# Another operation order and another PSUM bank table for a fused tokenizer, attention and feed-forward kernel

## The reference

```python
h = tok(x)                                   # 16x16 patches: layernorm(768), @ W (768x256) + b, layernorm(256) -> (64, 196, 256)
h = concatenate([h, txt], axis=1)            # (64, 273, 256)
h = h + attn(_layernorm(h), Wq, bq, Wk, bk, Wv, bv, Wo, bo)   # 16 heads of 16, over the 273 tokens reshaped by the projection
h = h + ffn(_layernorm(h), W_r, W_k, W_v, mu_r, mu_k)         # sigmoid(xr @ Wr.T) * (relu(xk @ Wk.T)**2 @ Wv.T), xr/xk mix each token with the one before
```

## Time and profile before

| | |
|---|---|
| median of 3 executions | 1610.56 us (1608.76 to 1613.27) |
| the profiled execution's own time | 1609.15 us |
| span in its trace | 1607.4 us, mean granted PE clock 0.968 |
| busy share | PE 90%, PEld 86%, DVE 79%, ACT 69%, POOL 59% |
| DMA | 227.67 MB moved, mean 142 GB/s |
| chain that ended last | PE 65%, SP queue 8%, issue 6%, DMA 5%, DVE 3% |

### The profile page before, as it was taken

One profiled execution on the slowest core, in us unless ns is written; L12 is line 12 of the kernel. 1 busy time (PEld: TensorE's weight loads), 2 busy tenths in 40 slices (PEclk: granted clock), 3 DMA queues, 4 the chain that ended last, 5 costly groups with the idle time before them and its releaser, 6 DMA issues.

```text
span 1607.4 us, 53715 instructions
## 1 busy us (share of the span) xinstructions
PE 1450.4 (90%) x18762; PEld 1378.2 (86%) x18762; DVE 1264.3 (79%) x3171; ACT 1113.4 (69%) x2230; POOL 947.0 (59%) x1428
## 2 busy tenths in 40 slices
PE   4687899999989999998999899999999999897866
PEld 4676899899989999898989899998988999897755
DVE  5566798888888888887988688888888788886753
ACT  4554687777777787776777678777777777765643
POOL 3342376566667666565667566666766566664546
PEclk8788899999999999999999999999999999999998
DMA  5267987997878887987888798798888689868760
GB/s 140 63 125 126 139 154 147 150 159 158 151 144 162 157 156 154 149 152 145 155 147 157 140 151 154 162 150 147 155 158 156 137 152 148 160 123 127 123 100 29
DMA packets 702660, 227.67 MB, mean 142 GB/s; under 512 B 617470, under 2 KB 673854, under 8 KB 702394
## 3 DMA queue, kind: packets, MB, share of 16 engines
q1 hardware_dynamic: 702394, 224.23, 77.3%
HBM read 121.64 MB, written 89.64 MB: 131 GB/s over the span
## 4 chain that ended last, share of the span: by engine, by line
PE 65%; SPq 8%; issue 6%; DMA 5%; DVE 3%; POOL 1%; ACT 1%; DVEq 0%; POOLq 0%; ACTq 0%
PE bank L1066 33%; PE bank L1146 13%; PE bank L1103 4%; PE bank L1124 4%; SPq L547 4%; DMA qk<-qkv_dram 3%; PE bank L1134 3%; SPq L519 2%; PE bank L1111 2%; PE bank L1180 2%; PE bank L1162 1%; PE bank L1194 1%; DMA on<-o_dram 1%; SPq L556 1%; PE bank L1153 1%
## 5 line engine op out<-in xcount | busy, mean ns | idle before, releaser
L1066 PE MATMUL bank<-wqkv,xnT 128*126 128x384 f32 (+1 forms) x1728 | 357.8, 347 | 6.9 <-issue 6.8
L1146 PE MATMUL bank<-wtok,xT 128*98 128x258 f32 x2304 | 315.7, 293 | 13.3 <-DVE xT L789 9.3
L1146 PEld LDWEIGHTS bank<-wtok,xT 128*98 128x98 f32 x2304 | 294.8, 172 | 18.9 <-DVE xT L789 11.3
L1066 PEld LDWEIGHTS bank<-wqkv,xnT 128*126 128x126 f32 (+1 forms) x1728 | 293.6, 186 | 10.6 <-issue 8.0
L689 POOL TENSOR_TENSOR mixp<-mixf,mixp 128x364 fp32r<-128x364 f32 x192 | 185.5, 977 | 166.0 <-ACT mixp L1040 158.7
L866 DVE TENSOR_TENSOR qkvt<-bank,bqkv 126x384 f32<-126x384 f32 (+1 forms) x288 | 156.0, 550 | 83.5 <-PE bank L1066 83.4
L954 ACT ACTIVATE arena<-qk,ymask 128x768 f32<-128x768 f32 x192 | 164.0, 926 | 57.1 <-DMA qk<-qkv_dram 56.9
L637 POOL TENSOR_TENSOR xcols<-xcols 84x896 f32<-84x896 f32 x59 | 124.9, 2117 | 86.9 <-ACT xcols L996 86.3
L987 ACT ACTIVATE xT<-bank 128x420 fp32r<-128x420 f32 (+1 forms) x192 | 100.5, 536 | 61.7 <-PE bank L1134 59.9
L1066 PE MATMUL bank<-wrT,mixp 128*126 128x256 f32 (+1 forms) x864 | 134.3, 292 | 4.8 <-POOL mixp L689 2.9
L979 ACT ACTIVATE xcols<-xim 84x640 f32<-84x640 f32 (+1 forms) x192 | 126.5, 694 | 12.9 <-DVE xs L784 12.0
(11 more groups left out here) (125 smaller groups left out, 3328.4 us busy)
## 6 DMA issues: line engine op xcount, KB each, us to landing
xim<-in_x SPq DMA_DIRECT2D x128, 294.0 KB
qk<-qkv_dram SPq DMA_DIRECT2D x48, 768.0 KB, 7.7
qkv_dram<-qkvt SPq DMA_DIRECT2D x96, 378.0 KB
arena<-qkv_dram SPq DMA_DIRECT2D x384, 48.0 KB
qkv_dram<-qkvt SPq DMA_DIRECT2D x48, 336.0 KB
o_dram<-probs SPq DMA_DIRECT2D x288, 48.0 KB, 1.8
out<-h SPq DMA_DIRECT2D x96, 126.0 KB
on<-o_dram SPq DMA_DIRECT2D x64, 126.0 KB
```

Source lines behind the costliest of these rows:

```text
L1066: ins = mm(psum, left(a, k), right(b, k), start=t == 0, stop=t == len(terms) - 1)
L1146: ins = mm(place("tok", c)[0:PT, 0:E + 2], xT[:, a, i0:i0 + GRID // 2, :].rearrange("p i w -> p (i w)"), wtok[:, b, ch, :], start=t == 0, ...
```

## The change

All numbers of `AT` and the bank table are replaced; no operation is added or taken away, and no other line differs. A few entries:

```diff
-    qk_in=[18794], v_in=[19932], qplace=[19665, 19706], kspread=[19343, 19395, 19463, 19541], s=[20021, 20045],
+    qk_in=[18898], v_in=[19971], qplace=[19751, 19776], kspread=[19643, 19763, 19798, 19801], s=[20013, 20066],
...
-BANK = dict(x=[5, 3, 1], tok=[3, 1], stat=[5], yn=[7], xt=[2, 0], qkv=[0, 5, 0, 2, 5, 0], s=[4, 2], pt=[4, 6],
-    av=[4, 6], ont=[5, 4], wo=[4, 6, 2], zt=[4, 6], k=[0, 6], r=[0, 2, 2], val=[0, 5, 0])
+BANK = dict(x=[5, 1, 3], tok=[1, 3], stat=[5], yn=[7], xt=[2, 0], qkv=[0, 6, 2, 6, 2, 5], s=[4, 0], pt=[0, 4],
+    av=[0, 4], ont=[4, 6], wo=[2, 0, 5], zt=[6, 4], k=[6, 5], r=[0, 2, 0], val=[5, 2, 0])
```

More of the change, by code:

```diff
@@ L69 @@
-BANK = dict(x=[5, 3, 1], tok=[3, 1], stat=[5], yn=[7], xt=[2, 0], qkv=[0, 5, 0, 2, 5, 0], s=[4, 2], pt=[4, 6],
-    av=[4, 6], ont=[5, 4], wo=[4, 6, 2], zt=[4, 6], k=[0, 6], r=[0, 2, 2], val=[0, 5, 0])
+AT = dict(load=[0], xcols=[1224, 1284, 1822], sq=[3222], ssq=[4012], sqm=[3868, 4648], x=[2111, 2157, 2217],
+    xh=[2208, 2548, 2596], xl=[2557, 2839, 2904], tok=[3197, 4151], stat=[4173], statc=[4624], statr=[4681],
+    rstd1=[4951], txt=[10645], yn=[5097, 5099], st2=[6096, 6315], mv2=[6643, 6685], rstd2=[7257], hg=[6820, 7574],
+    h=[7862, 7921], hdma=[10011], st3=[13135, 13155, 13226], mv3=[13379, 13508, 13546], rstd3=[13781], xn=[14022,
+    14047, 14108], xt=[14219, 14420], xnh=[14315, 14508], xnl=[14711, 14783], hb=[19860], qkv=[14829, 15408, 16006,
+    16508, 16656, 16783], qb=[15276, 16308, 16575, 16650, 16920, 16927], qkv_out=[17560, 17840, 17957],
+    qk_in=[18898], v_in=[19971], qplace=[19751, 19776], kspread=[19643, 19763, 19798, 19801], s=[20013, 20066],
+    mx=[20115, 20208], sub=[20217, 20226], exp=[20311, 20364], pt=[20322, 20439], ptc=[20380, 20503, 20544, 20547],
+    av=[20534, 20570], rec=[20658, 20794], osb=[20779, 20803], o_out=[21870], o_in=[26702], ont=[26847, 27034],
+    onh=[27090, 27115], onl=[27225, 27259], wo=[27328, 27808, 27964], h2=[27775, 27827, 28007], st4=[27781, 28258,
+    28409], mv4=[28434, 28488, 28541], rstd4=[28617], z=[28661, 28688, 28737], zt=[28824, 28862], carry=[25743],
+    ztc=[28832, 28931], d=[29081, 29255], edge=[29525], mix=[29673, 29832, 30289, 30531], mixh=[30009, 30013, 30808,
+    31196], mixl=[30192, 30231, 31913, 32207], k=[30625, 30718], kr=[30665, 30810], ksq=[30944, 31094], kah=[31998,
+    32152], kal=[32640, 32705], r=[32873, 33212, 33441], rt=[33298, 33649, 33826], val=[33747, 33748, 34038],
+    rv=[34041, 34094, 34197], add=[34661, 34679, 35169], out=[35081, 35540, 37491], sqh=[3607])
```

14 lines of the change are left out of this document (removed).

## The result

| | before | changed |
|---|---|---|
| median | 1609.66 us (1606.57 to 1613.27, 4 executions) | 1635.23 us (1634.04 to 1647.14, 4) |
| ratio | | 1.0165, 95% interval 1.0122 to 1.0208 |
| the profiled execution | 1609.15 us, span 1607.4 | 1635.34 us, span 1633.6 |

The change makes the kernel 26 us slower. Five further executions in a later run gave 1636.99 us (1634.25 to 1642.3) and a ratio of 1.016 (1.0134 to 1.0186).

The account below looks back on a forecast made before the run. PE was taken to bound the kernel, with `s` of kind 0 set by the loop through DRAM. Waits of +0.45 us a quad gave +6 us, the ends -4: +2 in total, forecast 1612 us, range for 8 in 10 1590 to 1634.

Parts of the forecast that it names:

- What bounds the kernel: Whole run: PE is busiest, 1450.4 us; a new order can only change its idle time, 56 us in the middle.
- (1): Third qkv job ahead of `s`: 1.1 us of PE's work moves from behind `s` to beside the loop.
- (2): DRAM loop of kind 0, `hdma` out and load in ahead of `qk_in`: 22.15 us against 23.15, wait 1.25 instead of 3.37.
- (2), its last sentence: Kind 0, `hdma` behind `qk_in`: its data should be there for `h` on DVE, 3 us behind `qplace`; no cost counted.
- (3): DRAM loop of kind 1, with `hdma` and `txt` ahead of `qk_in`: 21.95 us against 20.6 of work, 1.35 us of wait.
- (5): From `s` to `pt` in kind 0, without the qkv job that filled PE: `pt` waits, 1.0 us a quad.
- (6): Fourth qkv job sharing bank 6 with the second: waits in kinds 0 and 1, 0.3 us a quad together.
- The ends: Start-up -2.5 us from the moved qkv job and -1.5 from DVE's order; the end 0; together -4 us.
- the load delays `qk_in`: Slower rival: all 2.6 us of the load's extra bytes fall on kind 0's landing, 1.8 us more a quad, 1636; chance 0.22.

Follow-up runs that it names:

- after_qkv_behind: The changed kernel with the third qkv job back behind `s` in PE's order, as in the kernel before: 1663.34 us, ratio 1.0224.
- before_hdma_behind_qk: The kernel before with `hdma` behind `qk_in` in kind 0 and, on DVE, the first `h` behind `h2`: 1589.49 us, ratio 0.9896.
- after_loops_cleared: The changed kernel with kind 0's load and kind 1's `hdma` ahead of `o_out`, and `v_in` ahead of `txt` and the second `out`: 1603.05 us, ratio 0.9957.
- after_again: The changed kernel itself, unchanged, run again for five executions: 1636.99 us, ratio 1.016.
- after_small_load: The changed kernel with the load ahead of `qk_in` in kind 0 cut to an eighth of its columns from the ninth image on: 1605.93 us, ratio 1.0007.
- before_qkv_qb_ahead: The kernel before with the third qkv job ahead of `s` and the first `qb` on DVE ahead of `qplace`: 1686.87 us, ratio 1.0477.
- before_qkv_ahead: The kernel before with only the third qkv job moved ahead of `s` in PE's order: 1674.55 us, ratio 1.0371.

## Why the prediction was wrong

The forecast was 1612 us with a range up to 1634, and the slower of the named rivals was 1636, from the load. It came to 1635.23. By its own steps:

- *What bounds the kernel.* Right: PE's work and clock did not change, and 16 of the 26 us are idle PE time in the middle.
- *(1) The qkv job costs nothing.* Not contradicted in this order (after_qkv_behind), but not at nothing: PE waits 5.4 us in the middle for `h2` ahead of it, 0.4 us a quad. In the kernel before, the same move cost 3.7% through its bank, so that it was cheap here is, as far as the runs tell, the work of the new bank, and not that the work only changes sides.
- *(2) Loop of kind 0.* The loop came to 21.71 us in chunk 18 against 22.15, and the waits ahead of `s` of kind 0 fell by 26.6 us in the middle: this gain was real. The extra bytes ahead of `qk_in`, put at 0.8 us, came to 1.7 in the landing (median of kind 0, 7.8 before and 9.6 after); the whole load costs 2.3 (7.3 with an eighth of it). Chunk 18, with a landing of 8.3 before and 9.0 after, hides this.
- *(2), its last sentence*, "The four DMAs of `hdma` behind `qk_in` are awaited by `h` on DVE, which stands 3 us behind `qplace`, and should be there." **This is the step that failed.** It asked who waits for `hdma`, and not who stands behind it in SP's order: `v_in`, whose delay is in no term of the sum. From `qk_in` to `v_in` the time went from 5.4 to 10.6 us in chunk 18. Some 2 us of it are the load's bytes (11.1 us in the median against 8.7 with an eighth of them) and the rest is `hdma`, the second `out` and `txt`. By my estimate `v_in` had 3.4 to 3.8 us of slack in kind 0: the last of it was issued 0.95 us ahead of `s`, `av` started 5.7 us behind `s`, and where `v_in` is late `av` starts 2.8 to 3.2 us behind its last issue. Now the last is issued 3.9 us behind `s`. `av` waits 19.8 us in the middle against 8.1, the largest part of what the sum missed. The move of `hdma` by itself isn't to blame: before_hdma_behind_qk has it and gained 17 us. It took `hdma`, the load's bytes, the second `out` and `txt` together, and with the last two behind `v_in` and the load away (after_loops_cleared) `av` hardly waits.
- *(3) Loop of kind 1.* 22.1 us against 21.95 (medians of kind 1 against the forecast), `qk_in` issued later (11.4 us) and landed sooner (7.2); `s` there waits 1.0 us a quad against 1.35.
- *(5) `pt`.* 9.6 us in 12 waits, 0.8 each, against 1.0. *(6)* No such wait; in its place one of 0.2 at `wo` for `onT`, in every quad, since `ont` stands right ahead of it. The text had named `wo` among the places where it counts nothing.
- *The ends.* -4 us at the start did not come: the first `s` idles PE 0.34 us instead of 4.34, but it starts 1.3 us later. The end, taken as 0, is +5.1 (3.5 in after_again), most of it from `r` behind `zt`.

Sum of the middle in PE's waits, forecast and measured against before: `s` and `ont` -11.5 and -9.0 us, `pt` +13.1 and +9.6, term (6) +3.9 and nothing; and in no term `av` +11.7 and the projections for `h2` and `onT` +8.6. That is about +6 forecast and +20.9 measured in these lines, and -2.5 in all others. The ends are +1.3 and +5.1 against -4.

The rival "the load delays `qk_in`" had the time nearly right and half of the mechanism: after_small_load shows that the load's bytes are worth 1.0165 - 1.0007 = 1.6%, 25 us. Part of that goes the rival's way, through `s` and `ont` of kind 0 (9.1 us in the middle, 0.7 a quad, where it had 1.8). The rest is at `av` (5.7 of kind 0) and at the places behind it, which the rival did not have. That its 1636 is so near is luck in part.

Open stays why the load's place gives only 6 to 11 us when its bytes give 25. Without them, DMA also has 0.51 MB less to move of the 149 GB/s x 92.83 us = 13.8 MB of a quad, and with the load ahead of `o_out`, `o_out` is 1.1 us late; what each is worth no run shows. Nor does a run of the changed kernel move `hdma`, the second `out` or `txt` of kind 0 alone to the other side of `qk_in` or `v_in`, so what each of them cost isn't separated. Of the 2.4 us a quad that before_qkv_qb_ahead has more than before_qkv_ahead, 1.5 are longer busy time of PE (89.4 us a quad against 87.9), at a granted clock of 0.97 in the middle against 1.00; why the clock was lower is open.

## What to carry to other kernels

When a transfer is moved in a queue, list everything that stands behind it up to the next wait and ask for each how much slack it had; the consumer of the moved transfer is only one of them. A bulk transfer belongs ahead of the stretch in which small transfers are awaited one after another, where it drains beside their waiting: here the load behind `o_out` delays what stands behind it by 2.0 to 2.3 us; ahead of `o_out` it delays that by 1.1 us in the changed kernel and by nothing in the kernel before. And an order on one queue is judged with the engine orders that it was made for: exchanged whole, each was worse with the other's, while three steps on SP turned a loss of 1.6% into a gain of 0.4%.
